# One tiled attention kernel: block 0 of the Q/K/V projection computed two tiles ahead

## The reference, cut to what matters

```python
B, S, HID = 32, 32, 512;  D, HQ, HK = 128, 32, 8;  L = 512 cached keys
q, k, v = x @ Wq.T, x @ Wk.T, x @ Wv.T            # 32, 8, 8 heads of 128
q, k = rope(rmsnorm(q, q_norm_w), pos), rope(rmsnorm(k, k_norm_w), pos)
k_all, v_all = concat(k_cache[block_table], k), concat(v_cache[block_table], v)
scores = where(valid, q @ k_all.T / sqrt(D), -1e30)
x = x + (softmax(scores) @ v_all) @ Wo.T
h = x @ A.T;  gates = top-2 softmax(x @ Wr.T + 5 * onehot(language))
x = x + x @ W.T + 2 * sum_e gates[e] * (h[e] @ B[e].T)
```

## Time and profile before

| | us |
|---|---|
| median of 3 runs | 1357.91 (1353.44 to 1358.74) |
| the profiled execution, its own time | 1363.13 |
| its span, first to last instruction | 1361.3 |
| PE busy | 1292.8 (95%) |
| PE weight loads busy | 1165.9 |
| POOL busy | 918.8 |
| DVE busy | 891.0 |
| ACT busy | 870.4 |

### The profile page before, as it was taken

How to read it: one execution, slowest core, us unless ns; L and a number is a source line. 1 busy time by engine, 2 the same in 40 slices (tenths; PEclk the granted TensorE clock), 3 DMA queues, 4 the chain that set the end, 5 groups by cost and what they waited for, 6 DMA issues and landing times. The chain is left out here.

```text
span 1361.3 us, 26516 instructions
## 1 busy us (share of the span) xinstructions
PE 1292.8 (95%) x8896; PEld 1165.9 (86%) x8896; DVE 891.0 (65%) x2237; ACT 870.4 (64%) x2412; POOL 918.8 (67%) x1129
## 2 busy tenths in 40 slices
PE   4899999999999999999899999999999999999999
PEld 3788888988889998888789888988888899988887
DVE  7766666667576666667766566666767666666744
ACT  5666666666666666666666666666766666666640
POOL 7776776777676776777677677767767676776600
PEclk9899999999999999999999999999999999999999
DMA  6665444546564545555666454455656455454511
GB/s 231 209 184 144 135 131 135 163 141 194 156 183 137 155 141 150 142 149 147 195 172 178 135 156 126 133 147 163 202 157 191 122 142 162 135 155 127 171 46 62
DMA packets 73301, 207.77 MB, mean 153 GB/s; under 512 B 12176, under 2 KB 12464, under 8 KB 73008
## 3 DMA queue, kind: packets, MB, share of 16 engines
q0 software_dynamic: 40960, 134.25, 34.8%
q1 hardware_dynamic: 31392, 69.53, 16.2%
q10 hardware_dynamic: 816, 2.29, 0.5%
HBM read 195.77 MB, written 12.36 MB: 153 GB/s over the span
## 5 line engine op out<-in xcount | busy, mean ns | idle before, releaser
L1144 POOL DMA_INDIRECT kv_rows<-in_kv,step_idx x512 | 517.6, 1011 | 166.4 <-issue 140.2
L695 ACT ACTIVATE soft<-soft,min_all 128x544 f32<-128x544 f32 x256 | 191.9, 750 | 249.9 <-DVE min_all L898 182.3
L469 PEld LDWEIGHTS O<-pT,kv_rows 128*128 128x128 f32 x2048 | 260.6, 191 | 24.3 <-ACT pT L682 10.0
L469 PE MATMUL O<-pT,kv_rows 128*128 128x128 f32 x2048 | 271.9, 276 | 7.0 <-ACT pT L682 6.1
L898 DVE CUSTOM_DVE_ANT_0 soft<-SX,mask 128x544 f32<-128x544 f32 x256 | 184.3, 720 | 139.0 <-PE SX L188 105.4
L188 PE MATMUL SX<-kT,qT_hi 128*128 128x288 f32 (+1 forms) x1024 | 223.1, 307 | 2.0 <-DVE qT_lo L932 2.0
L914 DVE TENSOR_TENSOR oT_lo<-O,oT_hi 128x128 fp32r<-128x128 f32 x256 | 74.3, 290 | 202.1 <-ACT oT_hi L689 162.4
L682 ACT ACTIVATE pT<-PT 128x640 f32<-128x640 f32 x256 | 180.2, 704 | 22.4 <-PE PT L458 18.9
L414 PE MATMUL KT<-ident,kv_rows 128*128 128x128 f32 x1024 | 159.0, 278 | 34.8 <-DVE kT L918 14.8
L918 DVE TENSOR_TENSOR kT<-KT,kT 128x512 fp32r<-128x512 f32 x256 | 175.2, 684 | 2.2 <-ACT kT L654 2.1
L1164 POOL TENSOR_TENSOR rstd<-meansq,minus_half 128x4 f32<-128x4 f32 (+1 forms) x96 | 100.2, 1044 | 108.7 <-DVE meansq L886 107.2
(11 more groups left out here) (209 smaller groups left out, 2471.4 us busy)
## 6 DMA issues: line engine op xcount, KB each, us to landing
mask<-mask_rows SPq DMA_DIRECT2D x64, 272.0 KB
stage<-in_wqkv SPq DMA_DIRECT2D x22, 512.0 KB
x_raw<-in_xT SPq DMA_DIRECT2D x32, 256.0 KB
kv_rows<-in_kv,step_idx POOLq DMA_INDIRECT x512
stage<-in_wo SPq DMA_DIRECT2D x16, 512.0 KB
y_tile<-y_running SPq DMA_DIRECT2D x32, 256.0 KB
y_running<-y_tile SPq DMA_DIRECT2D x31, 256.0 KB
out<-kv_rows SPq DMA_DIRECT2D x8, 256.0 KB, 2.0
```

Source lines behind the costliest of these rows:

```text
L469: nc.tensor.matmul(O[:, 0:P], kv_rows[:, b, c, GK * D + h * D:GK * D + (h + 1) * D], pT[:, c * P:(c + 1) * P], start=c == 0, stop=False)
L695: nc.scalar.activation(probs[:, p % 2, 0:KEYS], scores[:, p % 2, :], ACT.Exp, bias=min_all[:, p:p + 1], scale=-1.0, accum_out=den[:, p:p + ...
L1144: G.indirect_dma_start(kv_rows[:, b, c, :], None, kv[:, :], bass.IndirectOffsetOnAxis(ap=step_idx[:, b * LC + c:b * LC + c + 1], axis=0)). ...
```

## The change

- PE runs blocks 1 and 2 of tile i+1 in pairs 0 to 3 (two chunks each) and block 0 of tile **i+2** in pairs 4 (one chunk), 5 (one) and 6 (two). Block 0 of tile 1 is done before the loop, after `score(0, 0)`.
- `split_x` works on halves of x (two chunks each): half 0 of tile i+2 at DVE's pair 3, half 1 at pair 5. The first waits for the new semaphore `x_used` (half 0 of x no longer read), the second for the third block.
- ACT and DVE follow: `take_block` at pairs 1, 3 (blocks 1, 2) and 6 (block 0 of i+2); `square_block` and `mean_square` at 0, 2, 4; `rotate` at 2, 4 and, for block 0 of i+2, after the last pair. ACT's `take_o_hi` goes ahead of `take_block`. `v_next` has two buffers.
- POOL gathers row 3 first in a tile, then makes the query table of tile i+1 and the key table of i+2, then takes the indices.
- SP loads x three tiles ahead, and the weight halves earlier (new `HI_AT`, `LO_AT`).

```diff
@@ -99,7 +99,7 @@
...
-        v_next = sb("v_next", [P, GK * D])
+        v_next = sb("v_next", [P, 2, GK * D])
...
@@ -203,8 +203,8 @@
...
-        HI_AT = ((6, 1), (6, 2), (6, 7), (7, 0), (7, 1), (7, 2), (0, 0), (0, 1), (0, 2), (0, 4))
-        LO_AT = ((6, 3), (6, 6), (6, 7), (7, 0), (7, 2), (7, 3), (0, 0), (0, 1), (0, 3), (0, 6))
+        HI_AT = ((6, 0), (6, 1), (6, 3), (6, 5), (6, 7), (7, 0), (0, 0), (0, 1), (0, 2), (0, 4))
+        LO_AT = ((6, 0), (6, 3), (6, 5), (6, 6), (7, 0), (7, 1), (0, 0), (0, 1), (0, 3), (0, 6))
...
@@ -246,15 +246,14 @@
...
-        def table_parts(t):
+        def table_parts(t, z):
...
-            for z in range(2):
-                for f in range(2):
...
+            for f in range(2):
...
@@ -319,10 +318,11 @@
...
-            sp.wait_ge(sm["x_ready"], 1)
+            sp.wait_ge(sm["x_ready"], 2)
             sp.dma_start(x_raw[:, :, :], xT[1, :, :].rearrange("p (c n) -> p c n", c=KC)).then_inc(sm["xT_in"], 16)
             next_half(0, 6)
             next_half(0, 7)
+            load_x(2, 2)
...
@@ -332,10 +332,6 @@
...
-                if fixed and t == TILES - 1 and not final:
-                    next_half(g + 1, 5)
-                if not (final and fixed and t >= TILES - 2):
-                    load_x(i + 2, (t + 2) % TILES if fixed else t + 2)
...
@@ -343,21 +339,25 @@
...
+                if not final and t == TILES - 2:
+                    next_half(g + 1, 2)
+                if not final and t == TILES - 1:
+                    next_half(g + 1, WO_FIRST)
+                    next_half(g + 1, WO_FIRST + 1)
                 if not last:
                     load_mask(i + 1, tn, 0)
-                if not final and fixed and t == TILES - 2:
-                    next_half(g + 1, 2)
+                if not final and t == TILES - 2:
                     next_half(g + 1, 3)
+                    next_half(g + 1, 4)
                 if before_last:
                     load_l1(2)
                     load_l1(3)
-                if not final and fixed and t == TILES - 1:
-                    next_half(g + 1, WO_FIRST)
-                    next_half(g + 1, WO_FIRST + 1)
                 if not last:
                     load_mask(i + 1, tn, 1)
-                if not final and fixed and t == TILES - 2:
-                    next_half(g + 1, 4)
+                if i + 3 < GROUPS * TILES:
+                    load_x(i + 3, (t + 3) % TILES)
+                if not final and t == TILES - 2:
+                    next_half(g + 1, 5)
...
@@ -390,16 +390,19 @@
...
-            def proj(i, k, part, wcount):
-
+            def proj(i, k, part):
+
+                wcount = i // TILES * HALVES
                 first, n = part
                 if first == 0:
-                    if k == 0:
-                        pe.wait_ge(sm["x_ready"], i + 1)
                     pe.wait_ge(sm["raw_ready"], i * NBLK + k)
+                if k == 0 and first % 2 == 0:
+                    pe.wait_ge(sm["x_ready"], 2 * i + first // 2 + 1)
                 if first % 2 == 0:
                     pe.wait_ge(sm["w_lo_ready"], wcount + 2 * k + (first + n - 1) // 2 + 1)
                 mm = three_pass(PROJ[:, :], xs, lambda c: (w_hi[:, k, c, :], w_lo[:, k, c, :]), n, first, KC - 1)
+                if first + n == KC // 2 and k == NBLK - 1:
+                    mm.then_inc(sm["x_used"], 1)
                 if first + n == KC:
                     mm.then_inc(sm["proj_done"], 1)
@@ -425,7 +428,7 @@
...
                 else:
-                    pe.wait_ge(sm["raw_ready"], i * NBLK + NBLK)
+                    pe.wait_ge(sm["raw_ready"], i * NBLK + NBLK + (i + 1 < GROUPS * TILES))
...
@@ -485,16 +488,18 @@
...
             turn_q(0, 0)
             turn_keys(0, 1)
             score(0, 0)
+            for half in halves:
+                proj(1, 0, half)
             turn_q(0, 1)
             score(0, 1)
             turn_keys(0, 2)
@@ -504,10 +509,10 @@
...
-                wcount = g * HALVES + (HALVES if end_of_group else 0)
-
-                fill = [[(0, c) for c in range(KC)], [(1, 0), (1, 1)], [(1, 2), (1, 3)],
-                        [(2, 0), (2, 1)], [(2, 2), (2, 3)], [], [], []]
+
+                fill = [[(i + 1, 1, 0), (i + 1, 1, 1)], [(i + 1, 1, 2), (i + 1, 1, 3)],
+                        [(i + 1, 2, 0), (i + 1, 2, 1)], [(i + 1, 2, 2), (i + 1, 2, 3)],
+                        [(i + 2, 0, 0)], [(i + 2, 0, 1)], [(i + 2, 0, 2), (i + 2, 0, 3)], []]
...
@@ -521,8 +526,9 @@
...
-                    for k, c in fill[p] if not last else []:
-                        proj(i + 1, k, (c, 1), wcount)
+                    for n, k, c in fill[p]:
+                        if n < GROUPS * TILES:
+                            proj(n, k, (c, 1))
...
@@ -625,8 +631,8 @@
...
                     nc.scalar.activation(raw[:, 0:GK * D], PROJ[:, 0:GK * D], ACT.Copy)
-                    act.wait_ge(sm["v_own_ready"], i)
-                    nc.scalar.activation(v_next[:, :], PROJ[:, GK * D:512], ACT.Copy).then_inc(sm["raw_ready"], 1)
+                    act.wait_ge(sm["v_own_ready"], max(i - 1, 0))
+                    nc.scalar.activation(v_next[:, i % 2, :], PROJ[:, GK * D:512], ACT.Copy).then_inc(sm["raw_ready"], 1)
...
@@ -751,6 +757,7 @@
...
             exponent(0, 0)
+            take_block(1, 0)
             act.dma_start(y_dram[:, :], x[:, :]).then_inc(sm["y_init"], 16)
             take_qT(0, 1)
...
@@ -767,8 +774,8 @@
...
-                    if not last and p in (1, 3, 6):
-                        square_block(i + 1, (1, 3, 6).index(p))
+                    if not last and p in (0, 2, 4):
+                        square_block(i + 1, p // 2)
...
@@ -784,12 +791,12 @@
...
-                    if p in (2, 4):
+                    if p != 6:
                         take_o_hi(i, p)
-                    if not last and p in (0, 2, 4):
-                        take_block(i + 1, (0, 2, 4).index(p))
-                    if p not in (2, 4, 6):
-                        take_o_hi(i, p)
+                    if not last and p in (1, 3):
+                        take_block(i + 1, p // 2 + 1)
+                    if p == 6 and i + 2 < GROUPS * TILES:
+                        take_block(i + 2, 0)
                     if not last and p == PAIRS - 1:
                         take_qT(i + 1, 1)
                         keep_v(i + 1)
@@ -855,20 +862,24 @@
...
-            def split_x(i):
+
+            def split_x(i, half):
+                part = slice(half * KC // 2, (half + 1) * KC // 2)
                 dve.wait_ge(sm["xT_in"], (i + 1) * 16)
-                if not (isinstance(i, int) and i == 0):
+                if half == 0:
+                    dve.wait_ge(sm["x_used"], i)
+                else:
                     dve.wait_ge(sm["proj_done"], i * NBLK)
-                    V.tensor_copy(x_hi[:, :, :], x_raw[:, :, :]).then_inc(sm["x_hi_ready"], 1)
-                dve.wait_ge(sm["x_hi_ready"], i + 1)
-                V.tensor_tensor(x_lo[:, :, :], x_raw[:, :, :], x_hi[:, :, :].bitcast(F32), ALU.subtract
+                V.tensor_copy(x_hi[:, part, :], x_raw[:, part, :]).then_inc(sm["x_hi_ready"], 1)
+                dve.wait_ge(sm["x_hi_ready"], 2 * i + half + 1)
+                V.tensor_tensor(x_lo[:, part, :], x_raw[:, part, :], x_hi[:, part, :].bitcast(F32), ALU.subtract
                                 ).then_inc(sm["x_ready"], 1)
...
-                dve.wait_ge(sm["table_ready"], (i + 1) * 8)
+                dve.wait_ge(sm["table_ready"], i * 8 + (4 if i > 0 and k == 0 else 8))
...
@@ -1000,6 +1013,8 @@
...
             rest_kT(0, 0)
+            split_x(1, 0)
+            split_x(1, 1)
             rest_qT(0, 0)
...
@@ -1010,10 +1025,10 @@
...
             normalise(0, 0)
-            split_x(1)
             rest_qT(0, 1)
             minimum(0, 1)
             rest_kT(0, 2)
+            rotate(1, 0)
             dve.wait_ge(sm["lang_in"], 16)
...
@@ -1039,23 +1054,23 @@
...
                     if not last:
-                        if p in (1, 2, 4):
+                        if p in (2, 4):
                             rotate(i + 1, p // 2)
...
-                        if p in (1, 3):
+                        if p in (0, 2, 4):
                             mean_square(i + 1, p // 2)
...
-                    if not last and p == 6:
-                        mean_square(i + 1, 2)
-                        if not (final and fixed and t >= TILES - 2):
-                            split_x(i + 2)
                     if not last and p == PAIRS - 1:
                         rest_qT(i + 1, 1)
                         minimum(i + 1, 1)
+                        if i + 2 < GROUPS * TILES:
+                            rotate(i + 2, 0)
+                    if p in (3, 5) and i + 2 < GROUPS * TILES:
+                        split_x(i + 2, p // 2 - 1)
...
@@ -1153,9 +1168,10 @@
...
-            def make_table(i, tn):
-                pool.wait_ge(sm["uv_ready"], i * NBLK)
-                for dst, a, w in table_parts(tn):
+
```

(46 more changed lines are left out.)

10 lines of the change are left out of this document (5 added, 5 removed).

## The result

The changed kernel takes **1379.24 us** (median; 1379.12 to 1380.05) against 1356.24 (1353.44 to 1358.74) before on the same chip: a ratio of 1.0178, 95% interval 1.0161 to 1.0194. It is slower by 1.8%, where I had forecast 1320 us. Its profiled execution has a span of 1377.3 us, 16.0 longer than before, at a granted clock of 0.999.

The account below looks back on a forecast made before the run. PE was taken to set the pace, so only its pauses could be won. The 20 ordinary tiles gave -21 us, the nine at group changes -15, the ends -2: -38 from 1357.9, so 1320 us, range 1302 to 1341.

Parts of the forecast that it names:

- the stock of pauses: PE's pauses that could be won: 29.3 us in the 20 ordinary tiles, 35.3 us in nine at group changes.
- The nominal pairs: PE's pair lengths without pauses after the chunks move: pair 4 at 3.54 us, pair 5 at 3.98.
- So that pause goes: Pair 6's 0.57 us pause before the KT transposes ends, as DVE gets 0.69 us more; 0.1 left per tile.
- My worry, pair 5: The KT pause might turn up again in pair 5, because pair 4 becomes short; bound 0.83 us per tile.
- The split, margins 0.1 and 0, taken as 0.15: PE's waits for x in pairs 4 and 6: DVE's halves just in time, 0.15 us together per tile.
- `take_block` ahead of `take_pT(7)`, 0.1: In pair 7 the copies before `take_pT(7)` just fit, leaving 0.1 us of pause per ordinary tile.
- POOL's earlier gather ends the waits for gathers: Row 3 gathered some 4 us earlier removes all gather waits: 0.17 us in pair 7, 2.15 in tile 7.
- The changes of group, -15: The nine tiles around a change of group gain 15 us, bounds -30 and +5, with 20 of 35.3 left.
- The ends, -2: 12 matmuls moved into PE's pause before the loop save 2.7 us, tile 30 costs 1: -2, bounds -3 and +2.
- Rival 1: The halves of x come 0.25 us late each, losing 15 us in 31 tiles: 1335 us, chance 0.17.
- Rival 4: Slower: half 0's lateness delays half 1 through three engines, about twice the lateness per tile: 1370 us, chance 0.04.
- its w of 0.8: The lateness of half 0, in us, at which the slower case gives 1370 us; break-even at 0.6.

Follow-up runs that it names:

- e4: e1, with half 0 of x also split before the rest of the new keys in pair 3: 1339.39 us, 0.9833.
- e5: Changed kernel with `normalise` also writing out an unread row sum, a form meant not to need the second port: 1358.58 us, 0.9971.
- e11: Changed kernel with the mean squares of the two query blocks a pair later on DVE: 1387.08 us, 1.0189.
- e1: Changed kernel with POOL's sum of the rotated queries also waiting until DVE has finished the normalisation that follows the rotation: 1371.59 us, 1.0076.
- e2: Kernel before the change, with only POOL's new order, row 3 gathered first in the tile: 1364.14 us, 0.9986.
- e3: Changed kernel with POOL's gather of row 3 back behind the tables and indices: 1383.59 us, 1.0160.
- e9: e1, with both halves of x split early in pair 3 and the summing form of `normalise` for `normalise(6)` alone: 1333.87 us, 0.9757.
- e6: Changed kernel with half 0 of x split before the rest of the new keys, POOL's sums not held: 1384.52 us, 1.0146.

## Why the prediction was wrong, point by point

- **PE sets the pace, and the stock of pauses:** right. The nominal pairs were right as well: unheld, pairs 4 and 5 take 3.53 and 3.99 us (e4), where I had 3.54 and 3.98.
- **"So that pause goes", of pair 6's KT transposes:** this step failed. It took DVE's durations from rows of the kernel before as constants. From `RECIPROCAL` at 515.75 to PE's start at 518.83 the round took 3.1 us, not 2.1; nearly all of the difference is `normalise(6)`, 1.57 us where that round of tile 10 had 0.64. That the pause goes when the hold goes is shown by e5 in part (0.6 to 0.3 us), by e11 (to 0.0) and by tile 19, not by e1, where the late `minimum(7)` takes its place. My worry, pair 5, has no pause (KT 0.55 after the pair's start).
- **The split, margins 0.1 and 0, taken as 0.15:** failed. For half 0 my sum of 1.6 us was right without POOL (1.46 in e1); in the changed kernel it ends 2.46 after pair 4's start, 0.7 late. For half 1 the margin itself was wrong: even in e4 it ends 2.1 after the pair's start, 0.4 late, behind `take_o(5)`, which waits 0.18 us for ACT's copy of O, and a `minimum(7)` that starts 0.27 late. The prediction had no sum for this half, only "the same". Together with the KT pause this is the failed part of the sum: two terms taken as 0.1 and 0.15 us for the ordinary tile measured 0.7 (KT: 0.1 in pair 4, 0.6 in pair 6) and 1.3 (x: 0.7 and 0.6).
- **`take_block` ahead of `take_pT(7)`, 0.1:** costs nothing; pair 7 takes 8.97 us against 9.00.
- **POOL's earlier gather ends the waits for gathers:** the waits in tiles 7, 15 and 23 are gone and tile 7 fell from 44.6 to 40.5 us, but the new order is not the cause: e2, with it alone, loses the wait for rows and gains nothing, as PE then waits for the weights; e3, with the rest of the change and the old order, takes 40.5 too. So the earlier weights were needed, and the order was not. A wait for rows of 1.94 us is new in pair 1 of tile 0. I didn't weigh that an earlier POOL also makes its arithmetic start earlier, beside other work of DVE.
- **The changes of group, -15:** -1 with the holds. In e9, which also splits x earlier, the nine tiles take 362.3 us, -12.7, so the term was nearly right but for these; no tile 6, 14 or 22 of the changed kernel is above 42.0 us.
- **The ends, -2:** about 0. Tile 0 took 2.0 more, which is its new wait for rows; tile 30 and the end took 1.8 less. In the filled pause the transposes took 0.63 us, at a granted clock of 1.00, where they had taken 1.11 at 0.50. This agrees with the rule that the prediction cited from the Trainium skill (TensorE: Matmul & The Clock Gate, "What's actually happening"), by which the gate follows how busy PE has been. But the loop begins at 41.4 us, as before (41.5), so nothing was won.
- **Rival 1** had the port in view, and looked only at the split. The Trainium skill (SBUF — State Buffer, "Who interferes with whom") says that `cast` and `tensor_scalar` between SBUF tensors can take the pair shared with GpSimd, not so the form that writes out its accumulator, and that a `tensor_tensor` with both inputs in SBUF meets GpSimd's reads. By that rule `normalise`, an instruction that the change doesn't touch, was the one to look at. The traces agree with each part: 1.57 us for `normalise`, 1.06 for the cast (e6), 1.17 for the subtraction (e1), and 0.78 at all times in the summing form (e5).
- **Rival 4** had the sign, and half of its mechanism: half 0 was late by about 0.7 and half 1 by 0.6, near its w of 0.8, and 1379 is near its 1370. I had excluded it because the split would need twice its time; the lateness stood in the queue ahead of the split, in `normalise(4)`.

So the total was nearly right for a kernel whose engines leave each other alone: e9, with the meetings mostly taken out and x split earlier, is 33 us faster than its kernel before, where I had 38, and 12 of its 20 ordinary tiles take 38.1 to 38.3 us, as I had said; the other eight take 38.8 to 39.7, so that by its trace the ordinary tiles give -12 where I had -21. The chance of 0.04 for slower was not right.

## What to carry to other kernels

When a change moves work in time, list beside each moved instruction what the engine that shares its memory port does in that moment; the duration in the old trace holds only for the old neighbours. A producer whose result releases a GpSimd operation should not have an SBUF-to-SBUF operation of VectorE right behind it: put one there that reads PSUM, or hold the release. And where a remedy alone gives nothing, look at where it pushed the collision before dropping the theory.
